# Attention rounds by half quads: maxima used two half-steps later, banks and side jobs rearranged

## What is computed

```python
x = x + attention_A(layernorm(x), ctx, ctx, mask)        # 16 heads of 16, keys and values are ctx; then W, b
x = x + ternary_ffn(layernorm(x))                        # Hadamard, rounding to 4 bits, ternary weights
x = x + attention_C(layernorm(x), ctx, bias)             # projections q, k, v, softmax with bias, W_o, then FFN with GELU, layer norm
x = x + experts(layernorm(x))                            # 8 experts, each takes its best 512 tokens
```

## Time and profile before

| what | us |
|---|---|
| median of 3 runs (lowest, highest) | 1172.48 (1169.89, 1172.68) |
| the profiled execution | 1171.72 |
| its span, first to last instruction | 1169.9 |
| busy: PE, DVE, ACT, POOL | 898.6, 625.2, 383.3, 281.3 |
| mean granted clock of PE | 0.876 of full |

### The profile page before, as it was taken

How to read it: one execution, slowest core, us unless ns; L and a number is a source line. 1 busy time by engine, 2 the same in 40 slices (tenths; PEclk the granted TensorE clock), 3 DMA queues, 4 the chain that set the end, 5 groups by cost and what they waited for, 6 DMA issues and landing times.

```text
span 1169.9 us, 17735 instructions
## 1 busy us (share of the span) xinstructions
PE 898.6 (77%) x7209; PEld 626.9 (54%) x7209; DVE 625.2 (53%) x1436; ACT 383.3 (33%) x589; POOL 281.3 (24%) x258
## 2 busy tenths in 40 slices
PE   3778777787887888789788788777674229999996
PEld 1334443454554555556455455555353228899985
DVE  3424555555565557556656655836421755667442
ACT  0212222222521522332252251231211005776663
POOL 2201110020012103103100210210121124777762
PEclk9968988888998898899889888898887558999998
DMA  9101532322332223233232232423000403555542
GB/s 299 44 23 32 207 137 84 132 104 80 129 137 85 95 101 135 95 111 129 77 127 104 77 113 87 184 91 141 21 17 22 142 19 95 131 127 136 147 82 25
DMA packets 47694, 120.55 MB, mean 103 GB/s; under 512 B 4736, under 2 KB 33920, under 8 KB 39424
## 3 DMA queue, kind: packets, MB, share of 16 engines
q1 hardware_dynamic: 41472, 111.06, 27.7%
q0 software_dynamic: 6144, 8.39, 4.0%
HBM read 111.05 MB, written 8.39 MB: 102 GB/s over the span
## 4 chain that ended last, share of the span: by engine, by line
PE 64%; DVE 19%; issue 6%; ACT 5%; POOL 2%; DMA 1%; SPq 0%; POOLq 0%; DVEq 0%; ACTq 0%
PE row_scores L320 12%; PE ps_x_C L396 6%; PE ps_x_A L396 5%; PE row_scores L1147 4%; DVE sum_inv L561 4%; PE ps_m L413 4%; PE ps_m L405 4%; PE row_scores L355 4%; PE ps_x_A L1164 3%; PE ps_x_C L1164 3%; PE ps_m L287 3%; DVE row_scores L536 3%; DVE probs L554 3%; DVE row_max_A L529 2%; PE key_scores L359 2%
## 5 line engine op out<-in xcount | busy, mean ns | idle before, releaser
L536 DVE CUSTOM_DVE_ANT_0 row_scores<-row_scores,bias_q 128x256 f32<-128x256 f32 x256 | 100.7, 456 | 133.0 <-PE row_scores L320 133.0
L710 ACT ACTIVATE probs<-probs 128x1024 f32<-128x1024 f32 x64 | 67.6, 1057 | 311.3 <-DVE probs L554 311.3
L529 DVE TENSOR_REDUCE row_max_A<-row_scores 128x4 f32<-128x1024 f32 x64 | 78.5, 1226 | 149.3 <-PE row_scores L355 149.3
L707 ACT ACTIVATE probs<-key_scores 128x1024 f32<-128x1024 f32 x64 | 65.5, 1024 | 212.4 <-PE key_scores L359 212.4
L320 PE MATMUL row_scores<-k_op_c,q_op_C 32*128 32x256 f32 x512 | 83.4, 447 | 52.0 <-DVE q_op_A L543 37.4
L320 PE MATMUL row_scores<-k_op_a,q_op_A 32*128 32x256 f32 x512 | 83.7, 448 | 46.0 <-DVE q_op_C L543 32.4
L320 PEld LDWEIGHTS row_scores<-k_op_c,q_op_C 32*128 32x128 f32 x512 | 52.6, 209 | 72.5 <-DVE q_op_A L543 43.6
L337 PE MATMUL key_scores<-q_op_A,k_op_a 32*128 32x256 f32 x512 | 86.9, 464 | 5.1 <-DVE q_op_A L543 4.0
L337 PE MATMUL key_scores<-q_op_C,k_op_c 32*128 32x256 f32 x512 | 83.3, 448 | 6.7 <-DVE q_op_C L543 6.7
L320 PEld LDWEIGHTS row_scores<-k_op_a,q_op_A 32*128 32x128 f32 x512 | 51.4, 204 | 66.7 <-DVE q_op_C L543 37.2
L554 DVE TENSOR_TENSOR probs<-key_scores,bias_k 128x1024 f32<-128x1024 f32 x64 | 77.9, 1217 | 12.0 <-PE key_scores L337 12.0
(11 more groups left out here) (230 smaller groups left out, 2089.1 us busy)
## 6 DMA issues: line engine op xcount, KB each, us to landing
bias_q<-in_bias_q SPq DMA_DIRECT2D x32, 1024.0 KB, 5.0
bias_k<-in_bias_k SPq DMA_DIRECT2D x32, 1024.0 KB, 4.9
w1e<-in_w1e SPq DMA_DIRECT2D x8, 1024.0 KB, 5.1
w2e<-in_w2e SPq DMA_DIRECT2D x8, 1024.0 KB, 6.3
k_op_a<-in_k_a SPq DMA_DIRECT2D x32, 128.0 KB, 2.2
mask_int<-in_mask SPq DMA_DIRECT2D x8, 512.0 KB, 5.6
v_op_A<-in_v_a SPq DMA_DIRECT2D x8, 512.0 KB, 5.6
w<-in_w SPq DMA_DIRECT2D x2, 1024.0 KB, 8.8
```

The lines of the kernel that those rows point to most:

```text
L529: nc.vector.tensor_reduce(of, row_scores[:, :, :].rearrange("p j (t k) -> p j t k", t=QT), AX_X, ALU.max).then_inc(max_taken, 1)
L536: ins = nc.vector.tensor_tensor_reduce(row_scores[:, j, qt * SEQ:(qt + 1) * SEQ], row_scores[:, j, qt * SEQ:(qt + 1) * SEQ], bias_q[:, m % ...
L707: nc.scalar.activation(of, key_scores[:, :, :], ACT.Exp).then_inc(exp_done, 1)
L710: nc.scalar.activation(of, of, ACT.Exp).then_inc(exp_done, 1)
```

## The change

A step is now half a position. In each step every engine does the work of one half: PE the round, the transposes of the maxima of the half-quad of the step before (into the new bank `ps_r`), at odd steps the values, then the side job; DVE take-maximum, bias, the addition of the maximum of the step before (64 partitions, the two heads of that half), the side job, at odd steps the normalisation. `group` swaps which two heads come first with each position, so that the heads whose maximum is taken in a half are those whose second pass is two steps later, and `then` and `now` stay in different row groups. The transposed operand rotates over three tiles per `par`. For A the mask matmuls come first in the round. The two banks `ps_x` become `ps_v` (values of both kinds, two projections, half of the FFN) and `ps_r`; keys of C and the router move to `ps_m[0]`. The normalisation keeps the reciprocal in `attnT`.

```diff
+MAX_TILE = {(q, half): (2 * [p for p in ORDER if p.par == q.par].index(q) + half) % 3 for q in ORDER for half in range(2)}
...
-        ps_x = {k: psum(f"ps_x_{k}") for k in (A, C)}
+        ps_v = psum("ps_v")
+        ps_r = psum("ps_r")
...
+        def group(quad, half):
+            return (PLACE[quad] - 1 + half) % 2
+
+        def previous_half(step):
+            pos, half = divmod(step - 1, 2)
+            return quad_of(pos + 1), half
...
         def pe_wait_maximum(pe, q, half):
-            n = number(q)
+            wait(pe, max_taken, half_number(q, half))
             if half == 0:
-                wait(pe, max_added, n)
...
         def pe_round(pe, now, then, half):
             if then is not None:
                 pe_wait_maximum(pe, then, half)
+                if then.kind == A:
+                    for n in range(2):
+                        pe_mask(row_scores[:, n, :], then, 0)
             if now is not None:
                 pe_wait_scores(pe, now, half)
+                if now.kind == A:
+                    for n in range(2):
+                        pe_mask(key_scores[:, n, :], now, 1)
+                pe.wait_ge(max_added, half_number(now, half) + 1)
...
+        def pe_maximum_rows(pe, q, half):
+            n = half_number(q, half)
+            pe.wait_ge(max_taken, n + 1)
+            wait(pe, max_added, n)
             for qt in range(QT):
+                ins = nc.tensor.matmul(ps_r[:, qt * P:(qt + 1) * P], row_max[q.par][MAX_TILE[q, half]][:, qt, :], ident[:, :],
                                        start=True, stop=True, is_transpose=True)
...
         def pe_values(pe, q):
...
-            wait(pe, norm_done, normalised_by(q.kind, pos - 1))
+            wait(pe, norm_done, chunk_number(q.kind, q.b, q.c))
...
         def pe_layers(pe):
+            for step in range(2 * FIRST, 2 * LAST):
+                pos, half = divmod(step, 2)
                 now, then, past = quad_of(pos), quad_of(pos + 1), quad_of(pos - 1)
+                maximised, of_half = previous_half(step)
                 if now is not None or then is not None:
+                    pe_round(pe, now, then, half)
+                if maximised is not None:
+                    pe_maximum_rows(pe, maximised, of_half)
+                if half == 1 and past is not None and past.par == 1:
+                    pe_values(pe, past)
+                pe_side(pe, *divmod(step, 16))
...
+        def ve_add_maximum(ve, q, half):
+            g = group(q, half)
+            r = slice(64 * g, 64 * g + 64)
+            ve.wait_ge(max_rows, half_number(q, half) + 1)
+            nc.vector.tensor_tensor(queries(q)[r, :], ps_r[r, 0:SEQ], queries(q)[r, :], ALU.add).then_inc(max_added, 1)
...
+            nc.vector.reciprocal(attnT[q.kind][:, q.c, :], ps_v[:, SEQ:2 * SEQ]).then_inc(inv_ready, 1)
             ve.wait_ge(inv_ready, n + 1)
+            nc.vector.tensor_tensor(attnT[q.kind][:, q.c, :], ps_v[:, 0:SEQ], attnT[q.kind][:, q.c, :],
...
         def ve_layers(ve):
...
+                if then is not None:
+                    ve_take_maximum(ve, then, half)
+                if now is not None and now.kind == C:
+                    ve_add_bias(ve, now, half)
+                if maximised is not None:
+                    ve_add_maximum(ve, maximised, of_half)
+                ve_side(ve, *divmod(step, 16))
+                if half == 1 and past is not None and past.par == 1:
                     ve_normalise(ve, past)
...
-            if s == 6 and p in BATCHES and p > 0:
+            if s == 11 and p in BATCHES and p > 0:
                 po_masks(po, p)
```

More of the change, by code:

```diff
@@ L75, in values_place, with values_step, normalised_by, jobs_before @@
     return PLACE[Quad(kind, b, 2 * c + 1)] + 1
[L78 to L85, removed]
+def values_step(kind, b, c):
+    return 2 * values_place(kind, b, c) + 1
+def normalised_by(step):
+    return sum(values_step(*k) <= step for k in CHUNKS)
+def jobs_before(step, first):
+    return sum(16 * b + first < step for b in BATCHES)
 def wait(eng, sem, value):
@@ L333, in pe_wait_scores, with pe_scores, pe_mask @@
                 pe.wait_ge(bias_added, 2 * C_NUMBER[before] + 2 - half)
-        def pe_scores(q, half, j, kb):
+        def pe_scores(q, j, kb):
             r = slice(32 * j, 32 * j + 32)
             return nc.tensor.matmul(key_scores[:, j % 2, kb * SEQ:(kb + 1) * SEQ], keys(q)[r, kb * P:(kb + 1) * P],
-                                    queries(q)[r, :], start=(kb == 0), stop=(q.kind == C and kb == QT - 1))
+                                    queries(q)[r, :], start=(q.kind == C and kb == 0), stop=(kb == QT - 1))
+        def pe_mask(bank, q, way):
+            nc.tensor.matmul(bank, ident_b[:, :], mask_bf[:, q.b % 2, way, :], start=True, stop=False)
         def pe_round(pe, now, then, half):
@@ L401, in pe_f1 @@
         def pe_f1(pe, f, n):
-            bank = ps_m[1] if n % 2 == 0 else ps_x[C]
+            bank = ps_m[1] if n % 2 == 0 else ps_v
             for hc in (2 * n, 2 * n + 1):
@@ L448, in pe_side @@
+            if s == 4 and f in BATCHES:
+                wait(pe, S["x1_ready"], jobs_before(step, 2))
+                pe.wait_ge(norm_done, normalised_by(step))
+                wait(pe, S["gelu_done"], 2 * jobs_before(step, 45))
+                pe_token_major(ps_v, attnT[C], w_o, S["wo_out"])
+            if s == 5 and r in BATCHES:
                 pe.wait_ge(S["hb_T_copied"], r + 1)
@@ L526, in ve_take_maximum @@
             first = DK * (1 - q.par)
-            of = row_max[q.kind][q.par][:, :, :].rearrange("p t (j r) -> p j t r", j=4)[:, 2 * half:2 * half + 2, :, first]
+            g = group(q, half)
+            of = row_max[q.par][MAX_TILE[q, half]][:, :, :].rearrange("p t (j r) -> p j t r", j=4)[:, 2 * g:2 * g + 2, :, first]
             if q.kind == A:
```

279 lines of the change are left out of this document (124 added, 155 removed).

## The result

The changed kernel takes **1067.16 us** (median of four runs, 1066.8 to 1067.7) against 1171.18 for the kernel before on the same chip: ratio 0.912, 95% interval 0.909 to 0.915. The profiled execution has a span of 1065.6 us against 1169.9, at a mean granted clock of 0.907 against 0.876.

A forecast was written before the change was run, and what follows sets the result against it. PE was taken to bound the kernel. A full batch was 73.3 + 7.6 + 3.5 = 84.4 us against 98.8; all stretches together gave -107, so 1171.7 - 107 = 1065 us, range 1028 to 1128.

The forecast's parts named there:

- clock: Two new groups of PE waits per full batch (step 6; steps 11 and 12) lower PE's clock, costing 3.5 us.
- C alone: Stretches with only kind C (138.6 us): addition leaves the normalisation's shadow (6.2), keys and FFN stop following values (about 8): -14.
- the start: Up to 144.1 us, with kind A alone, where DVE's share is small: -4 us, between 0 and -10.
- Floor of PE: PE's own work per full batch: 80.6 us busy, less 9.1 at full clock, plus 1.8 for more transposes: 73.3.
- New waits: PE's waits over the 16 steps of a full batch, at steps 2, 6, 10, 11, 12 and two more: 7.6 us.
- Masks: POOL's 3.65 us mask conversion moves from step 6 to 11, beside layer norm C: 0, ends -0.9 and +3.2 per batch.
- the stretch before: The stretch after the three full batches, 93.8 us with one position without kind A: -13 us.
- the one on banks: Sharing ps_v makes a chunk's values wait for the normalisation before; chunks about 9 us apart leave room for 3.59 + 2.1.
- A (DVE's order): Rival: DVE's strict order delays take-maximum, 0.5 to 0.9 us on ten steps per batch: 1100 to 1128 us; chance 0.17.
- B: Rival: mask conversion on POOL blocks DVE wholly on the path, 3.2 us on six batches: 1084 us; chance 0.11.
- C: Rival: the 16 steps run in series, 2.1 us uncovered each, 107 us per batch: slower, 1229 us; chance 0.07.
- D: Rival: an equal wait for take-maximum replaces the removed one, row_scores being one buffer: 1172 us; chance 0.05.

The follow-up runs named there:

- e9: The changed kernel with e4, e6, e7 and the copy for the router's logits on DVE instead of ACT, all together: 1038.6 us, ratio 0.889.
- e12: The changed kernel with six useless matmuls ahead of the transposes of the maxima at steps 6 and 11 of the first seven batches: 1046.3 us.
- e4: The changed kernel with POOL's mask conversion moved back from step 11 to step 6: 1066.4 us, ratio 0.913.
- e7: The changed kernel with half of the FFN of the last three batches in bank ps_r instead of ps_v: 1057.2 us, ratio 0.905.
- e2: The changed kernel with DVE's normalisation put back ahead of the addition of the maximum and the side job: 1135.1 us, ratio 0.969.
- e3: The changed kernel without the two-step lag, with transposes and addition at the end of the step that takes the maximum: 1117.6 us, ratio 0.957.
- e10: The changed kernel with the edits of both e2 and e3, no lag and the normalisation in front: 1140.9 us, ratio 0.976.
- e1: The kernel before, with DVE's addition of the maximum swapped ahead of the normalisation and nothing else changed: 1109.8 us, ratio 0.948.
- e5: The changed kernel with a second, useless addition of the same size on DVE ahead of each real one: 1090.8 us, ratio 0.932.
- e6: The changed kernel with the last quarter of the second FFN product on PE moved from step 5 to step 6: 1059.5 us, ratio 0.907.

## Why the prediction was right

**The sum.** 1065 was forecast, 1067.2 measured, and by stretches too: none is off by more than 3.3 us, and the two batches before the full ones came out at 73.8 and 79.9 us where 74 and 80 were put. Inside three of the terms, clock, C alone and the start, errors cancelled, which was luck.

**Floor of PE, 73.3 us.** Right: with the clock at 1.00, e9 shows 73.0 for the same matmuls (24 records missing in three batches), and e12, with no record missing, 73.4.

**New waits, 7.6 us; clock, 3.5.** Measured idle time is 6.9 (6.0 if all the missing records lie in it), and 76.5 - 73.0 = 3.5 is the clock's part. The waits are right place by place: behind step 6, 1.4 + 1.1 for 2.5; step 11, 1.9 for 1.8; logits 1.2 for 1.5; steps 2 and 10, 0.4 and 0.4 for 0.6 each. What PE still waits for follows from the written order, and could be counted. The clock's part is right as a sum alone. Two groups of waits per batch were each to cost half of it. Behind step 6 the clock fell in one of the three batches only; behind steps 11 and 12 it fell in all three, and half of the whole loss of the three batches is one stretch of 10 us at 0.50, from 508.4 on. The 8 us behind step 6 in the first two batches, then the stretch from 508.4 on:

```profile
316.40:324.40 8.00, 7.95 (x95) 4.27 (x100) 6.99 (x13) 2.24 (x4) 3.13 (x4) 0.79 0.28 97
400.10:408.10 8.00, 7.95 (x113) 5.05 (x115) 7.77 (x14) 3.48 (x6) 3.12 (x4) 1.00 0.27 89
508.40:518.64 10.24, 10.12 (x48) 7.04 (x52) 3.33 (x12) 3.42 (x4) 0.78 (x1) 0.50 0.51 154
```

**Additions of 64 partitions, 0.42 us.** Right: 0.43 (row at 486.92), so half the partitions don't make one cheaper.

**Masks, 0.** Right by e4, and layer norm C stood as foreseen; that at step 6 they delay the quantiser was not. One reading of the earlier trace rows was off: it was the second half of layer norm R that stood (486.96 to 488.32), while the first took 0.41 us.

**C alone, -14, and the stretch before, -13.** Too hopeful: -10.9 and -10.3. The stretch before idles 8.4 us (83.48 - 75.04), 1.5 more than a full batch, and the prediction gave it no waits of its own. With C alone the step that failed is the one on banks, "two chunks lie two steps (about 9 us) apart, and 3.59 + 2.1 fits": it looked at the normalisation before the values, and left out GELU's read of the same bank, 8.0 us by the list of waits and 8.2 by e7. That it is only 3 us off is because the rest of the term was too small by about 5. Nor is that rest confirmed in its parts. Its "about 8" doesn't follow from the pieces named for it: 3.59 + 2.1 + 4.2 - 4.5 is 5.4. And the 6.2 us of waits for the addition did not go: in this stretch 16.2 us of PE's idle time end with the addition (the list under e7), where it was 6.2 and these 3.7 before (721.44 to 903.19):

```profile
PE row_scores L320 <- DVE q_op_C L543: 3.7, 5, 1.0
```

What went there are other waits, and no run takes them apart.

**The start, -4.** The sum came out (-3.4), its parts didn't: from the first projection to the second the changed kernel takes 6.0 us longer than before (58.54 against 52.57). There the transposes of layer norm C wait 4.1 us, beside a mask conversion, a mask matmul waits 1.5 for that conversion, and the clock is 0.85 where it was 0.92. I had no term for this stretch's own waits. The way to the first projection, 9.4 us shorter, makes up for it; it alone differs by some 4 us between the changed kernel and e7, which are the same up to there.

**The mechanism.** The prediction costed lag and order as one edit and credited the steps' minimum. The square of e2, e3 and e10 confirms that they work as one (7 and 22 us alone, 74 together); e1 shows what it did not say, that 60 of the 104 us were to be had from swapping two statements in the old kernel.

**The rivals.** A (DVE's order): take-maximum is PE's releaser at one place of a full batch (1.4 us), not in most steps, and e5 shows a quarter of added DVE time on the path there, not all of it. B: excluded by e4, in which PE's waits at steps 11 and 12 are the same. C: e3, which puts the transposes behind the side jobs of the same step, is as near as a run came to it, and a full batch is then 90.8 us, not 107. D is excluded by the result.

## What to carry to other kernels

Two late operations in front of the same round hide each other's price: read DVE's timeline for what stands ahead of the instruction that PE waits for, and try its order first, since that is two lines. Where one engine bounds, count a batch as floor, listed waits and clock, and put the reader of every shared PSUM bank on the list, not just the last writer. A wait of 1 to 2 us in the bounding engine can cost more in clock than in idle time (1.9 us at step 11, then once 9 us at a clock of 0.51, which is 4.4 us lost); whether it does is seen by filling it with work of no use.

## What the hardware showed that was not expected

**The same wait doesn't always lower the clock.** The 1.95 us at step 11 (1.94 in places), in four batches of each of seven kernels, was followed in the next 8 us by a clock of 1.00 in none of four in the changed kernel and in e7, one of four in e4, e5 and e6, and three of four in e2 and e9. Two windows behind this wait in e9, the second slow, and the one in the changed kernel:

```profile
496.90:504.90 8.00, 8.00 (x66) 6.11 (x66) 5.33 (x23) 5.30 (x7) 0.00 (x0) 1.00 0.73 213
575.20:583.20 8.00, 8.00 (x37) 5.86 (x36) 3.60 (x14) 3.47 (x4) 0.00 (x0) 0.57 0.52 164
```

```profile
508.19:517.19 9.00, 8.88 (x37) 5.96 (x36) 3.54 (x12) 3.62 (x4) 0.99 (x1) 0.51 0.58 175
```

At 0.57 and 0.51 most of the window is at the lower level, 1.2 GHz. What in the surroundings decides was not tried.

**Only the two ends of POOL's conversion hold DVE.** In e6 q_scale (128 x 2) ends at 472.89, as POOL's addition does (472.86). In e4 it took 0.64 us instead of 0.17 beside the mask conversion, but the reciprocal behind it 0.17 as ever, with POOL's instruction still running for 2.4 us. In the changed kernel one layer norm C wasn't held at all, in the middle of a conversion:

```profile
183.06 3.65 POOL L830 TENSOR_SCALAR mask_bf<-mask_int 128x1024 bf16<-128x1024 int32 x1
184.97 0.73 DVE L609 TENSOR_SCALAR nrm_C<-x_all,mv_C,rstd_C 128x256 f32<-128x256 f32 x2
```

All halves of layer norm C and all q_scale that meet a conversion of 3.65 us, in the traces of all kernels, fall into three groups. Those that began less than 0.5 us behind its start (or just ahead of it) ended 1.06 to 1.18 us behind that start; those that began 1.1 to 2.3 us behind it took what they take alone (0.41 and 0.17); those that began from 2.5 to 3.3 us behind it stood until 0.14 us behind its end. So the middle of this conversion holds nothing, and whether a DVE instruction beside it is dear depends on when it begins.

**Transposes became dearer**: 315 ns of mean duration against 292 to 296 for the same shape before (lines 386 and 369), the median 327 against 273. They now stand right behind the round. In e3 and e10, where they stand at the end of the step, the median is 273 again: the price goes with the place. The prediction had taken the old duration.
